# Half weight loads, low weights spread over heads, and another bank for the key rotation in the first batch of an attention and mixture-of-experts kernel

## The reference

```
h = take(weight, ids)                                # 8 x 512 x 256
x = layernorm(h)
q, k, v = x @ w_aq, x @ w_ak, x @ w_av               # 8 heads of 128
q, k = rope(q), rope(k)
p = softmax(q k^T / 128 - 1e30 * (i < j))
h = h + sum over heads of (p v) @ w_ao
h = h + moe(layernorm(h))                            # 8 experts, 1024 rows each
```

## Time and profile before

| | |
|---|---|
| Time, median of 3 runs | 1201.84 us (1199.5 to 1203.94) |
| The profiled execution's own time | 1200.93 us |
| Its span, first to last instruction | 1198.7 us |
| Busy share of the span | PE 95%, PEld 83%, POOL 69%, DVE 68%, ACT 60% |
| Mean granted TensorE clock | 0.985 of full speed |
| First query product of batch 0 | 19.23 us |
| First query product of head 3 | 49.58 us |

### The profile page before, as it was taken

How to read it: one execution, slowest core, us unless ns; L and a number is a source line. 1 busy time by engine, 2 the same in 40 slices (tenths; PEclk the granted TensorE clock), 3 DMA queues, 4 the chain that set the end, 5 groups by cost and what they waited for, 6 DMA issues and landing times. The chain is left out here.

```text
span 1198.7 us, 20289 instructions
## 1 busy us (share of the span) xinstructions
PE 1142.1 (95%) x7083; PEld 999.6 (83%) x7083; DVE 818.8 (68%) x1972; ACT 720.7 (60%) x1533; POOL 825.4 (69%) x926
## 2 busy tenths in 40 slices
PE   3899999999999999999999998878999999999997
PEld 2788888888888888888888885558999999999996
DVE  4787887887887887887887766854555554554433
ACT  3667677677686686676676765315465555555642
POOL 3897898897897897897997864052484574654425
PEclk9999999999999999999999999789999999999999
DMA  5000100100100100100101003321362442523223
GB/s 197 1 18 2 45 28 1 45 27 1 45 27 2 45 28 1 54 18 9 63 1 36 19 1 112 110 66 39 94 138 32 115 124 32 130 39 104 32 23 36
DMA packets 42213, 58.12 MB, mean 48 GB/s; under 512 B 8896, under 2 KB 34944, under 8 KB 41984
## 3 DMA queue, kind: packets, MB, share of 16 engines
q0 software_dynamic: 13824, 21.24, 9.9%
q1 hardware_dynamic: 28288, 35.58, 8.8%
HBM read 35.71 MB, written 16.91 MB: 44 GB/s over the span
## 5 line engine op out<-in xcount | busy, mean ns | idle before, releaser
L278 ACT ACTIVATE prob<-prob,row_min 128x512 f32<-128x512 f32 (+3 forms) x256 | 141.8, 557 | 108.3 <-DVE row_min L468 108.3
L1322 DVE TENSOR_TENSOR hT_lo<-hid,hT_hi 128x512 fp32r<-128x512 f32 x124 | 86.2, 695 | 172.9 <-ACT hT_hi L1498 156.1
L1495 ACT ACTIVATE hid<-up,b_e 128x512 f32<-128x512 f32 x128 | 88.1, 688 | 158.9 <-PE up L1650 138.7
L214 POOL TENSOR_TENSOR q_sin<-q_sin,rope_t 128x512 f32<-128x512 f32 x64 | 82.8, 1293 | 84.0 <-ACT q_sin L302 84.0
L206 POOL TENSOR_SCALAR prob<-prob,row_inv 128x512 f32<-128x512 f32 (+3 forms) x256 | 134.5, 540 | 7.9 <-DVE row_inv L481 5.9
L1036 POOL DMA_INDIRECT x<-routed_rows,tokens x64 | 80.7, 1262 | 79.6 <-DVE tokens L1316 38.1
L403 DVE TENSOR_TENSOR pT_lo<-bank,pT_hi 128x384 fp32r<-128x384 f32 (+1 forms) x192 | 110.7, 596 | 18.4 <-ACT pT_hi L260 17.2
L1047 POOL TENSOR_SCALAR y<-y,gate 128x256 f32<-128x256 f32 x60 | 32.2, 548 | 127.1 <-issue 126.3
L1056 POOL DMA_INDIRECT out<-y,tokens x60 | 98.6, 1643 | 16.2 <-issue 13.9
L682 PE MATMUL bank<-ident,prob 128*128 128x128 f32 x640 | 101.9, 274 | 4.8 <-POOL prob L206 4.7
L260 ACT ACTIVATE pT_hi<-bank 128x384 fp32r<-128x384 f32 (+1 forms) x192 | 96.4, 518 | 13.6 <-PE bank L682 13.3
(11 more groups left out here) (318 smaller groups left out, 3887.9 us busy)
## 6 DMA issues: line engine op xcount, KB each, us to landing
raw<-in_w SPq DMA_DIRECT2D x16, 1024.0 KB
emb_res<-emb SPq DMA_DIRECT2D x8, 512.0 KB, 3.8
out<-h SPq DMA_DIRECT2D x8, 512.0 KB, 2.9
routed_rows<-x SPq DMA_DIRECT2D x8, 512.0 KB, 3.0
x<-in_wq SPq DMA_DIRECT2D x1, 1024.0 KB
x<-in_wk SPq DMA_DIRECT2D x1, 1024.0 KB, 5.1
x<-in_wv SPq DMA_DIRECT2D x1, 1024.0 KB, 7.3
x<-in_wo SPq DMA_DIRECT2D x1, 1024.0 KB, 10.2
```

The lines of the kernel that those rows point to most:

```text
L278: nc.scalar.activation(pr, pr, ACT.Exp, bias=row_min[:, h % 2, k:k + 1], scale=-1.0, accum_out=row_sum[:, h % 2, k:k + 1]).then_inc(s["exp ...
L1322: nc.vector.tensor_tensor(out, in_, hi.bitcast(F32), ALU.subtract)\
L1495: nc.scalar.activation(hid[:, t % 2, :], up_ps[t % 2][:], ACT.Gelu, bias=bias)
```

## The change

In batch 0 alone, and in what leads to it:

- The loads of wq, wk and wv are split in two halves of 512 columns (a: heads 0 to 3, b: heads 4 to 7). SP's order is ids, q a, identity, mask, k a, rope, a wait for the four gathers, v a, v b, q b, k b, wo, wr.
- Each gather of batch 0 has a semaphore of its own. DVE takes the statistics of a block when it has landed, with the low part of q a behind the second. Each normalised block counts, and PE transposes block by block (`first_xt`) into the score banks.
- ACT forms the high parts of q a and k a, the mask, v a, then xT, then v b; q b and k b follow behind head 0's swap, wo in two halves behind the swaps of heads 1 and 2.
- POOL forms the low part of v a, behind the reciprocal root.
- DVE forms the low part of k a ahead of xT's, that of v b in heads 0 and 1, those of single heads of q and k (4 in head 2; 5, 6, 7 behind the last minimums of heads 3, 4, 5), and wo's one head at a time behind the last minimums of n = 2 to 9.
- For n < 3 (`FIRST`) the key's sine products go to a PSUM bank (5, or 6 for n = 2), and DVE instead of POOL sums the rotation there and forms the key's low part; ACT takes the key's high part ahead of the query's.
- PE's first query product puts its terms with xT's low part last. The values of heads 0 to 2 go to banks 6 and 7 and no longer wait for swap and key rotation; the q and k products of heads 1 to 3 wait for these instead of for the values' low part.
- PE runs filler products of 384 columns on the mask row (`warm`) while it waits in the opening, and four behind head 0.

```diff
@@ SP
+            load("q", "a")
+            sp.dma_start(ident[:], a["ident"][:, :]).then_inc(s["ident_in"], 16)
+            sp.dma_start(mask_f, a["mask"][:, :]).then_inc(s["mask_in"], 16)
+            load("k", "a")
+            sp.dma_start(rope_t[:], a["rope"][:, :, :]).then_inc(s["rope_in"], 16)
+            for tb in range(TB):
+                sp.wait_ge(s[f"first_emb{tb}"], 16)
+            load("v", "a")
+            load("v", "b")
+            load("q", "b")
+            load("k", "b")
@@ POOL
             rsqrt(0)
+            pool.wait_ge(s["w_hi"], 3)
+            pool.wait_ge(s["xn_ready"], 1)
+            nc.gpsimd.tensor_tensor(piece(w_qkv["v"][1], "a"), piece(wraw["v"], "a"),
+                                    piece(w_qkv["v"][0], "a").bitcast(F32), ALU.subtract)\
+                .then_inc(s["va_lo"], 1)
...
+                    if live and n < FIRST:
+                        low(b, h, "q")
+                    elif live:
                         add(b, h, "k")
                         low(b, h, "q")
                         low(b, h, "k")
@@ ACT
+            split_high("q", "a")
+            split_high("k", "a")
+            act.wait_ge(s["mask_in"], 16)
...
+            split_high("v", "a")
             xt(0)
+            split_high("v", "b")
...
                         swap(b, h)
+                    if b == 0 and h == 0:
+                        split_high("q", "b")
+                        split_high("k", "b")
+                    if b == 0 and h in (1, 2):
+                        act.wait_ge(s["wo_in"], 16)
+                        hi_of(w_o[0][:, 4 * h - 4:4 * h], wraw_o[:, 4 * h - 4:4 * h], "w_hi")
...
+                    if live and n < FIRST:
+                        qk_high(b, h, "k")
@@ DVE
+            def add_k(b, h):
+                n = b * H + h
+                after(dve, "k_rope", n + 1)
+                nc.vector.tensor_tensor(k_bank(n)[:], k_cos[:], k_bank(n)[:], ALU.add)\
+                    .then_inc(s["k_add"], 1)
...
+            for tb in range(TB):
+                dve.wait_ge(s[f"first_emb{tb}"], 16)
+                nc.vector.bn_stats(stats[:, tb, :], emb[:, tb, :]).then_inc(s["stats_done"], 1)
+                if tb == 1:
+                    split_low("q", "a", 1)
+                if tb > 0:
+                    dve.wait_ge(s["stats_done"], tb)
+                    nc.vector.bn_aggr(mean_var[:, tb - 1, :], stats[:, tb - 1, :])
...
             first_normalise()
+            split_low("k", "a", 2)
             xt(0)
...
                         turn_k(b, h)
+                        if n < FIRST:
+                            add_k(b, h)
...
+                    if n < 2:
+                        value_low(n)
+                    if n == 2:
+                        head_low(4, "q")
+                        head_low(4, "k")
+                    if n < FIRST:
+                        low_k(b, h)
...
                         minimum(b, h - 1, 2)
                         minimum(b, h - 1, 3)
                     side_work(b, h, len(slots) == H, 1)
+                    if 2 <= n < 2 + H:
+                        wo_low(n - 2)
+                    if b == 0 and 3 <= h <= 5:
+                        head_low(h + 2, "q")
+                        head_low(h + 2, "k")
@@ PE
+                elif b == 0 and h < 4:
+                    after(pe, "q_swap" if x == "q" else "k_rope", n)
                 elif x == "q":
                     after(pe, "v_lo", 2 * TB * b + V_SLOT[h - 1][-1] + 1)
...
-                after(pe, "k_rope" if i else "q_swap", n + 1)
+                if b == 0 and h < 3:
+                    after(pe, "v_lo", h)
+                else:
+                    after(pe, "k_rope" if i else "q_swap", n + 1)
...
+            pe.wait_ge(s["mask_zero"], 1)
+            pe.wait_ge(s["ids_in"], 16)
+            warm(12)
+            for tb, n in enumerate((4, 4, 4, 2)):
+                pe.wait_ge(s[f"first_emb{tb}"], 16)
+                warm(n)
+            pe.wait_ge(s["aggr_done"], 1)
+            warm(4)
+            pe.wait_ge(s["rstd_done"], 1)
+            warm(3)
+            pe.wait_ge(s["ident_in"], 16)
+            first_xt()
...
+                        if n == 0:
+                            first_project()
...
+                    if n == 0:
+                        warm(4, s_ps[0])
```

More of the change, by code:

```diff
@@ L128, in build_attention, with piece, k_bank, v_bank @@
         rows_b = a["rows"].rearrange("(b p) m -> p b m", p=P)
+        def piece(x, part):
+            return x[:, :, 0:H * D // 2] if part == "a" else x[:, :, H * D // 2:H * D]
+        def k_bank(n):
+            return r_ps[0] if n == FIRST - 1 else bank[5]
+        def v_bank(b, h, i):
+            return r_ps[i if h == 0 else h - 1] if b == 0 and h < 3 else proj_ps[i]
         @block.sync
         def _(sp):
+            def load(k, part):
+                sp.dma_start(piece(wraw[k], part), piece(wsrc[k], part)).then_inc(s[f"w{k}{part}_in"], 16)
             sp.dma_start(ids[:], a["ids"][0]).then_inc(s["ids_in"], 16)
[L133 to L139 removed]
+            load("q", "a")
[9 more added lines that the diff above has]
+            load("k", "b")
             sp.dma_start(wraw_o, a["wo"].rearrange("h d m -> d h m")).then_inc(s["wo_in"], 16)
@@ L158, in body @@
                 after(sp, "r_evac", b)
[L159 removed]
+                after(sp, "emb_in", b * 16 * TB)
                 sp.dma_start(emb_res[:], emb[:]).then_inc(s["res_in"], 16)
@@ L294, in qk_high @@
                 after(act, "s_done", 3 * (n - 2) + 3)
-                hi_of(out[0][:, h % 2, :], cos[:], f"{x}_hi")
+                hi_of(out[0][:, h % 2, :], k_bank(n)[:] if x == "k" and n < FIRST else cos[:], f"{x}_hi")
             def swap(b, h):
@@ L332, in normalise2 @@
                 after(act, "shift2_done", b + 1)
-                if isinstance(b, int) and b == 0:
+                if b == 0:
                     act.wait_ge(s["w_lo"], 4)
+                    act.wait_ge(s["va_lo"], 1)
+                    act.wait_ge(s["qb_lo"], H // 2)
+                    act.wait_ge(s["kb_lo"], H // 2)
+                    act.wait_ge(s["wo_lo"], H)
                 for tb in range(TB):
@@ L406, in stats_of @@
             def stats_of(b, blocks):
-                after(dve, "emb_in", (b + 1) * 16 * TB)
+                after(dve, "emb_in", b * 16 * TB)
                 for tb in blocks:
@@ L420, in first_normalise, with split_low, value_low, head_low @@
                 for tb in range(TB):
-                    last = nc.vector.tensor_scalar(xn[:, tb, :], emb[:, tb, :], mean_var[:, tb, 0:1],
-                                                   rstd[:, tb:tb + 1], ALU.subtract, ALU.mult)
-                last.then_inc(s["xn_ready"], 1)
+                    nc.vector.tensor_scalar(xn[:, tb, :], emb[:, tb, :], mean_var[:, tb, 0:1],
+                                            rstd[:, tb:tb + 1], ALU.subtract, ALU.mult)\
+                        .then_inc(s["xn_ready" if tb == TB - 1 else "first_xn"], 1)
+            def split_low(k, part, hi):
+                after(dve, "w_hi", hi)
+                low_of(piece(w_qkv[k][1], part), piece(wraw[k], part), piece(w_qkv[k][0], part), "w_lo")
+            def value_low(kt):
+                after(dve, "w_hi", 4)
+                x = [piece(w, "b")[:, kt, :] for w in (w_qkv["v"][1], wraw["v"], w_qkv["v"][0])]
+                low_of(*x, "w_lo")
+            def head_low(h, k):
+                after(dve, "w_hi", 5 if k == "q" else 6)
+                at = slice(h * D, (h + 1) * D)
+                low_of(w_qkv[k][1][:, :, at], wraw[k][:, :, at], w_qkv[k][0][:, :, at], f"{k}b_lo")
+            def wo_low(h):
+                after(dve, "w_hi", 7 + h // 4)
+                low_of(w_o[1][:, h, :], wraw_o[:, h, :], w_o[0][:, h, :], "wo_lo")
+            def add_k(b, h):
[3 more added lines that the diff above has]
+                    .then_inc(s["k_add"], 1)
+            def low_k(b, h):
+                n = b * H + h
+                after(dve, "k_hi", n + 1)
+                low_of(kT[1][:, h % 2, :], k_bank(n)[:], kT[0][:, h % 2, :], "k_lo")
             def shift_of(b):
@@ L623, in products, with warm, first_xt, first_project @@
                 return last
+            def warm(n, at=o_ps):
+                for _ in range(n):
+                    nc.tensor.matmul(at[:, 0:3 * P], mask_row[:, 0:P], mask_row[:, 0:3 * P],
+                                     start=True, stop=True)
+            def first_xt():
+                for tb in range(TB):
+                    after(pe, "first_xn" if tb < TB - 1 else "xn_ready", tb + 1 if tb < TB - 1 else 1)
+                    for kt in range(KT):
+                        last = nc.tensor.transpose(s_ps[kt][:, tb * P:(tb + 1) * P],
+                                                   xn[:, tb, kt * P:(kt + 1) * P], ident[:])
+                        if tb == TB - 1:
+                            last.then_inc(s["xt_tr"], 1)
+            def first_project():
```

(12 more changed lines are left out.)

82 lines of the change are left out of this document (35 added, 47 removed).

## The result

| | before | after |
|---|---|---|
| median of the runs, us | 1200.97 (1198.68 to 1203.94, 5 runs) | 1192.47 (1189.87 to 1195.88, 5 runs) |
| profiled execution, its span | 1200.93, 1198.7 | 1191.39, 1189.6 |
| start of head 3's query product | 49.58 | 42.00 |
| start of head 63's | 694.58 | 688.74 |
| from there to the end of the span | 504.1 | 500.9 |

A forecast was written before the change was run, and what follows sets the result against it. PE bounds the kernel (95% busy), so only the stretch before head 3 can give time. 8.9 us gained there, less the give-back, nets 5.8 to 6.2, taken as 6.0: 1194.9, as a median 1195.8, range 1191.5 to 1200.3.

The forecast's parts named there:

- The opening: Before head 0: statistics per gather and halved weights bring q_cos of head 0 to 17.6, 5.8 us earlier.
- The mean is there at 11.0: Opening, DVE: only one statistics instruction and one aggregate behind the last gather, so the mean at 11.0, not 12.2.
- the four gathers at the same 10.28: Opening: all four gathers landed at 10.28 as in the kernel before, since POOL issues them as before.
- the rival of halves that don't land apart: Opening: first values' half lands only with the full MB, ACT holds up xT; 2.2 gained, 1199.6; chance 0.12.
- adds short products during the wait: Opening, PE: the change's short products during the wait, set against the chance of a half-speed engine clock.
- Heads 0 to 2: Values in output banks, head 1 at 21.9, then DVE with ACT the bound; head 3 at 40.7, 8.9 us less.
- The clock: Rival: PE at 1.2 GHz at 15.7, twelve q and k products 2.4 us longer; 3.6 gained, 1198.2; chance 0.18.
- I take no fall: Gaps ahead of head 3: new PE gaps are at most 1.5 us, so the granted clock doesn't fall.
- one would cost little: Ahead of head 3: a fall of the granted clock would cost little, since DVE leads there.
- The give-back: Heads 3 to 5: low-weight pieces on DVE and POOL operations hold each other off; 3.1 us lost, or 2.7 if POOL pays.
- Nothing given back: Rival, heads 2 to 9: pieces find POOL idle or finish in DVE's waits; 8.9 gained, 1192.9; chance 0.24.
- The slower case: Rival, heads 2 to 9: 16 pieces each wait a full POOL operation, 26.2 against 8.9; 1219.1, half 1206; chance 0.08.

The follow-up runs named there:

- q_low_first: Changed kernel with the low part of wq's first half on DVE moved ahead of all statistics; 1184.5 us, ratio 0.9941 to the kernel before.
- three_together: Changed kernel with ten opening fillers, wq's first low part ahead of the statistics, and low-weight pieces behind the turns' low halves; 1185.91 us, ratio 0.9952.
- no_fillers: Changed kernel with all filler products of the attention part left out; 1188.17 us, ratio 0.9971 to the kernel before.
- fewer_fillers: Changed kernel with 10 instead of 21 filler products behind the gathers; 1187.19 us, ratio 0.9965 to the kernel before.
- after_again: Changed kernel run once more without edit; 1193.32 us, ratio 0.9951 to the kernel before.
- lows_by_memset: Changed kernel with the spread low pieces of wq, wk and wo in heads 2 to 9 set to zero by memset; 1192.53 us, ratio 0.9938.
- lows_after_turns: Changed kernel with the low-weight pieces moved to the end of a head's DVE work; 1184.48 us, ratio 0.9943 to the kernel before.
- k_rotation_on_pool: Changed kernel with FIRST = 0, the first three heads' key rotation and low part back on POOL; 1185.4 us, ratio 0.995.

## Why the prediction was right, and where its steps were not

The forecast for attention was a net 6.0, and 5.8 came (5.7 and 6.4 in the two other pairs). The median lies 3.3 below the forecast. Of that 0.9 is the kernel before, whose median over five runs is 1200.97 and not the 1201.84 from which the forecast was made; the medians differ by 8.5, that is 2.5 more than the 6.0. The prediction didn't count a shorter tail (3.3 in the profiled pair, 2.15 and 1.3 in the others), and the tails of the variants show that it goes with the executions. That the median still fell into the range, 1.0 above its lower end, is partly luck. The net of attention is right partly by offsetting errors, too.

*The opening.* "The mean is there at 11.0" is the step that failed: it came at 12.7. Two terms make up the 1.7. I left wq_lo, which the diff puts between the statistics, out of their sum: in the kernels that have it elsewhere the mean is 1.1 us nearer to the first landing. And I counted "the four gathers at the same 10.28", but the last one was there only at 10.8 (10.2 before; 11.7 against 10.0 and 11.2 against 10.1 in the two other pairs). Why the changed kernel's gathers land later, though POOL issues them at the same times, no run shows. The rest of the step held: with wq_lo out of the way (q_low_first, three_together) the mean comes 0.8 us behind the last gather, where 0.7 was counted and the kernel before took 2.0, so the statistics per gather do save their 1.2. Normalise was to run 12.7 to 14.1 and ran 14.39 to 15.77. The half of the value weights landed at 14.5 (14.0 to 14.1 expected), and ACT had it ready when the transposes ended, so the rival of halves that don't land apart fell. A second thing was missing: the fillers, which I named as what "adds short products during the wait" and gave no time. They hold the transposes until 16.05, 0.3 us behind the last normalise. q_cos of head 0 was to be at 17.6 and stood at 19.45, 3.95 earlier than before and not 5.8.

*Heads 0 to 2.* Head 1 was to start at 21.9 and did at 23.84, the same 1.9 late. Its rotation came at 26.52 (24.85), head 2's at 34.36 (33.0), head 3's products at 42.00 (40.7). So 0.6 us of the delay was absorbed in between, and the working of these heads was sound: 7.6 gained at head 3 against 8.9.

*The clock.* The rival (0.18) fell. The first products are 0.23 apart, the pace of 2.4 GHz. That it was a real danger is shown by no_fillers and fewer_fillers, which lose 2 to 3 and 1.5 us. "I take no fall" for the gaps ahead of head 3 held in the first execution and not in after_again (0.74); "one would cost little" is borne out there, for from head 3 to head 8 that execution needed 54.06 us against 53.97.

*The give-back.* Right in kind, too large in size, and spread otherwise. In head 3 the pieces were to take until 54.8, and q_cos came at 55.45, 3.03 behind head 4's first product (52.42), where 3.65 was forecast. The first and the third piece were to wait and the second not; it was the second that did (1.50 us), the first waited 0.2 and not 1.3, and the third not at all, beside the issue of a gather. Between heads 3 and 6 it is 32.46 us against 31.35: 1.1 given back, where 3.1 was forecast; 0.8 more follows in head 6, and all is over by head 8. That the pieces cause it is shown: with memsets heads 4 to 7 take 10.2 to 10.5 us each, 1.98 less in all, and 1.34 less than in after_again, whose head 3 was slow as well. That it is their wait for POOL rather than their length is seen in single rows only, since the move behind the turns shortened the pieces and brought nothing. Of POOL's side only the kT_both of 1.48 us is seen, no wait for prob.

A rule of the Trainium skill (SBUF — State Buffer, Who interferes with whom) stood in the prediction: a DVE instruction with two inputs from SBUF and a GpSimd instruction that reads SBUF exclude each other, and the order of issue decides. The 0.62, 1.50 and 1.48 agree with it. The third piece shows where it ends: beside an instruction that issues a gather (53.95, 1.10) the piece took 0.42, no longer than in head 5 with nothing of POOL's in its way. What failed in the give-back is therefore not the rule but my count of what POOL has to do at that moment.

*The other rivals.* Nothing given back (1192.9) would be 7.6 and not 5.8 at head 63; it names nearly the measured total, but for a wrong reason. The slower case needed a third of 26.2 us unhidden, and 7% was.

So two errors nearly cancel: 1.3 us too much at head 3, and 2.9 given back behind it where it was 1.8.

## What to carry to other kernels

When an engine is kept busy with filler work for its clock, the fillers have a length, and a faster supplier gains nothing until they end: put their last row beside the row that they wait for. Their number is a trade, here 21 that end 0.3 us behind what they cover (in executions where they ran faster they ended before it, and head 0 started some 0.7 us sooner), against ten that lost the clock and 1.5 us. Read the gain from the start of each repeated stage, and compare the untouched tail on its own before a total is believed; here it swung by 1.4 us on one chip and by 9 to 10 from the first chip to the third. Compare an experiment with a run that has the same granted clock just ahead: here most of one edit's seeming saving was a slow head before the stretch. The time that a small piece of two-input work takes depends on its neighbour on the other engine as well as on its size: 0.41 us alone, 1.50 beside an operation of 1.3.

## What the hardware showed that was not expected

- The kernel before took 1200.55 us on one chip and 1192.0 and 1192.1 on two others. On the two of these chips on which it was profiled the difference lies behind attention: head 63 starts at 695.15 and 695.46, with 504.15 and 494.4 us behind.
- POOL's first small operation for the root (four elements a partition) took 0.91 us instead of 0.24 beside a two-input operation of DVE, the mirror image of the shift of the earlier trace rows.
- A piece of 256 columns on DVE takes 0.41 us alone with two SBUF inputs, and 0.27 as a memset.
- The length of PE's gap doesn't tell when the granted clock falls. Over 41 to 47 us it was 0.72 in lows_by_memset, behind a gap of 1.04 us, and also 0.72 in lows_after_turns, behind one of 0.66, and 0.74 in after_again, which is the changed kernel itself; in the first execution of that kernel a gap of 0.64 at the same place was followed by 1.00. k_rotation_on_pool had gaps of 1.20 at 36.36 and 1.39 at 41.53 and kept 1.00 from there to 94 us.
- Four gathers of 128 rows, issued by POOL 1.3 to 1.4 us apart, landed 0.31 to 0.35 us apart (9.76 to 10.75 in the first execution of the changed kernel, 11.0 to 12.0 in q_low_first).
